# A wait for the stores of the new x moves from the end of the experts' stage to the state space's first load of a residual

## The reference

```
x = x + ga * attention(h)                      # layer 0, first half
h = layernorm(x) * (1 + cb) + sb
x = x + gb * experts(h)                        # layer 0, second half: gives the "new x"
h = layernorm(x) * (1 + ca) + sa               # layer 1
x = x + ga * state_space(h)                    # layer 1, first half
h = layernorm(x) * (1 + cb) + sb
x = x + gb * permuted_mlp(h)                   # layer 1, second half
```

## Time and profile before

| what | value |
|---|---|
| median of 3 runs | 1777.32 us (1776.28 to 1777.55) |
| the profiled execution's own time | 1780.89 us |
| its span on the core | 1779.1 us |
| PE busy | 1490.2 us (84%) |
| DVE busy | 1322.9 us (74%) |
| ACT busy | 1134.0 us (64%) |
| POOL busy | 924.0 us (52%) |
| DMA queue q1 (SP) | 163.81 MB, 34.3% of 16 engines |

### The profile page before, as it was taken

How to read it: one execution, slowest core, us unless ns; L and a number is a source line. 1 busy time by engine, 2 the same in 40 slices (tenths; PEclk the granted TensorE clock), 3 DMA queues, 4 the chain that set the end, 5 groups by cost and what they waited for, 6 DMA issues and landing times. The chain is left out here.

```text
span 1779.1 us, 26522 instructions
## 1 busy us (share of the span) xinstructions
PE 1490.2 (84%) x9052; PEld 815.1 (46%) x9052; DVE 1322.9 (74%) x2126; ACT 1134.0 (64%) x2277; POOL 924.0 (52%) x603
## 2 busy tenths in 40 slices
PE   5888999999978895678688898998989888755668
PEld 2441222222246443556365575665657566422432
DVE  3339999999056414107999999999999999999232
ACT  2323777777922233347788878878887887855138
POOL 0000000001010223326999999999999999999303
PEclk9875999999965897699799899999999999866689
DMA  6411112221072345823354554555554554644112
GB/s 247 160 43 42 28 32 81 79 81 59 3 231 95 101 137 206 290 69 87 96 137 114 132 136 118 129 122 118 135 130 119 125 125 108 137 101 112 68 51 95
DMA packets 154386, 199.10 MB, mean 112 GB/s; under 512 B 17567, under 2 KB 124999, under 8 KB 152716
## 3 DMA queue, kind: packets, MB, share of 16 engines
q1 hardware_dynamic: 142252, 163.81, 34.3%
q0 software_dynamic: 5168, 18.63, 3.2%
q10 hardware_dynamic: 6832, 14.96, 2.3%
HBM read 151.08 MB, written 46.28 MB: 111 GB/s over the span
## 5 line engine op out<-in xcount | busy, mean ns | idle before, releaser
L2040 DVE TENSOR_TENSOR_SCAN shared<-ssm_psum,ssm_state,shared 128x256 f32<-128x256 f32 x1024 | 674.9, 722 | 20.7 <-ACT ssm_state L1927 12.2
L1940 ACT ACTIVATE ssm_psum<-shared,ssm_a 128x256 f32<-128x256 f32 x1024 | 443.6, 468 | 157.7 <-DVE shared L2040 151.3
L1662 POOL TENSOR_TENSOR shared<-shared,ssm_bc 128x1024 f32<-128x1024 f32 x256 | 509.3, 2000 | 35.4 <-DVE shared L2040 16.0
L734 ACT ACTIVATE att_probs<-att_psum 128x1024 f32<-128x1024 f32 x256 | 248.3, 1021 | 75.2 <-PE att_psum L661 72.6
L1639 POOL TENSOR_TENSOR shared<-shared,ssm_bc 128x1024 f32<-128x1024 f32 x144 | 287.9, 1999 | 12.2 <-DMA shared<-drive_rows 12.2
L775 DVE TENSOR_REDUCE att_rowmax<-att_psum 128x1 f32<-128x512 f32 x448 | 277.5, 681 | 3.3 <-PE att_psum L634 1.5
L1765 PE MATMUL ssm_psum<-shared,ssm_select 128*32 128x256 f32 x2048 | 170.4, 423 | 93.9 <-POOL shared L1662 93.3
L603 POOL COPY att_v<-v_tokens 128x128 f32<-128x128 f32 x8 | 2.3, 292 | 298.8 <-ACT att_out L728 298.8
L634 PE MATMUL att_psum<-att_k,att_q 32*128 32x512 bf16 x448 | 138.0, 398 | 9.9 <-DVE att_rowmax L775 7.3
L1700 PE MATMUL ssm_psum<-ssm_h,late_weights 128*128 128x256 f32 x512 | 133.0, 421 | 9.3 <-ACT shared L1900 5.4
L673 PE MATMUL att_psum<-att_probs,att_v 128*32 128x512 f32 x1024 | 137.2, 608 | 0.6 <-ACT att_probs L734 0.6
(11 more groups left out here) (261 smaller groups left out, 1822.3 us busy)
## 6 DMA issues: line engine op xcount, KB each, us to landing
shared<-drive_rows SPq DMA_DIRECT2D x256, 256.0 KB, 4.5
qkv_wmod<-in_wmod SPq DMA_DIRECT2D x8, 1536.0 KB, 12.3
shared<-in_x SPq DMA_DIRECT2D x8, 1024.0 KB, 5.1
late_weights<-in_we SPq DMA_DIRECT2D x8, 1024.0 KB, 13.4
ssm_bc<-bc_rows SPq DMA_DIRECT2D x32, 256.0 KB, 5.2
drive_rows<-ssm_delta SPq DMA_DIRECT2D x64, 128.0 KB, 1.7
drive_rows<-ssm_du SPq DMA_DIRECT2D x64, 128.0 KB, 1.8
sorted_results<-moe_y ACTq DMA_DIRECT2D x23, 256.0 KB, 2.0
```

The lines of the kernel that those rows point to most:

```text
L734: nc.scalar.activation(probs[:, u % RING, :].rearrange("p (j t) -> p j t", j=2), ps_s[u % 2], ACT.Exp).then_inc(exp_done, 1)
L1662: nc.gpsimd.tensor_tensor(read(Q), drive(Q), bc[:, c % 2, 1, gr, :].unsqueeze(1).to_broadcast([P, J, SW]), ALU.mult).then_inc(read_done, 1)
L1940: nc.scalar.activation(ps_decay[n % HALF_BANKS][:, i], rep[:, s % 2, 0, j, :], ACT.Exp, scale=amat[:, t, gr, j:j + 1]).then_inc(decay_done, 1)
L2040: nc.vector.tensor_tensor_scan(drive(Q)[:, j, :], ps_decay[(2 * Q + j // 2) % HALF_BANKS][:, j % 2], drive(Q)[:, j, :], state[:, t, gr, j: ...
```

## The change

SP's block in `experts` no longer ends with the wait for the stores of the new x. The semaphore `x2_stored` becomes one of the shared ones, made in `build`, and `load_residual` waits for it before the first load.

```diff
--- before.py
+++ after.py
@@ -917,8 +917,8 @@
         srt_in = [sem(f"sorted{i}_in") for i in range(LOADS)]
         y_stored = [sem(f"y{i}_stored") for i in range(YSLOTS)]
         back_in = [sem(f"back{i}_in") for i in range(BACKS)]
-        x2_done, x2_stored, stat2_done, var2_done, sd2_done, rstd2_done, shift2_done, hn_dve, hn_act, hn_mm, hn_out = (sem(n) for n in (
-            "x2_done x2_stored stat2_done var2_done sd2_done rstd2_done shift2_done hn_dve hn_act hn_mm hn_out").split())
+        x2_done, stat2_done, var2_done, sd2_done, rstd2_done, shift2_done, hn_dve, hn_act, hn_mm, hn_out = (sem(n) for n in (
+            "x2_done stat2_done var2_done sd2_done rstd2_done shift2_done hn_dve hn_act hn_mm hn_out").split())
         block = ctx.enter_context(nc.Block())
         hdram = scratch.h.rearrange("(t p) f -> p t f", p=P)
         xdst = scratch.x2.rearrange("(t p) f -> p t f", p=P)
@@ -957,10 +957,9 @@
                 sp.dma_start(we[:, e], d["we"][e].rearrange("(k p) m -> p k m", p=P)).then_inc(experts_in, 16)
             for i in range(SCH):
                 sp.wait_ge(x2_done, (i + 1) * TC)
-                sp.dma_start(xdst[:, i * TC:(i + 1) * TC], x[:, i * TC:(i + 1) * TC]).then_inc(x2_stored, 16)
+                sp.dma_start(xdst[:, i * TC:(i + 1) * TC], x[:, i * TC:(i + 1) * TC]).then_inc(g.x2_stored, 16)
                 sp.wait_ge(hn_out, (i + 1) * TC)
                 sp.dma_start(hdst[:, :, i * SW:(i + 1) * SW], hnt[:, i % TSLOTS]).then_inc(g.hn_stored[i % TSLOTS], 16)
-            sp.wait_ge(x2_stored, 16 * SCH)
 
         @block.gpsimd
         def _(pool):
@@ -1567,6 +1566,8 @@
                     sp.dma_start(rep[32 * n:32 * n + 32, s % 2], src).then_inc(rep_in[s % 2], 16)
 
             def load_residual(c):
+                if c == 0:
+                    sp.wait_ge(g.x2_stored, 16 * SCH)
                 if c >= 1:
                     sp.wait_ge(out_mm, c * MP)
                 sp.dma_start(xres[:], xsrc[:, c * ST:(c + 1) * ST, :]).then_inc(xres_in, 16)
@@ -2231,6 +2232,7 @@
         g.att_used = []
         g.win_in = [ctx.enter_context(nc.semaphore(f"{n}_in")) for n in ("win_inner", "win_gate", "wout")]
         g.hn_stored = [ctx.enter_context(nc.semaphore(f"hn{s}_stored")) for s in range(TSLOTS)]
+        g.x2_stored = ctx.enter_context(nc.semaphore("x2_stored"))
         g.out_stored = [ctx.enter_context(nc.semaphore(f"out_{b}_stored")) for b in ("even", "odd")]
         g.ident = sb("ident", [P, P])
         g.run = sb("shared", [P, 2 * KT * T])
```

## The result

| | kernel before | changed kernel |
|---|---|---|
| median of 6 runs | 1777.18 us (1773.88 to 1779.87) | 1782.74 us (1778.22 to 1785.21) |
| span of the profiled execution | 1779.1 us | 1781.4 us |

The ratio is 1.0026, with a 95% interval from 1.0014 to 1.0038: slower by 4.6 us, or 2.5 to 6.8.

A forecast was written before the change was run, and what follows sets the result against it. The prediction took VectorE to hold the state space, so only its start matters; the load of h, sharing engines with the gate load, adds 4.0 us, other terms 0: 1777.32 + 4.0 = 1781.3 us, range 1776.3 to 1783.0.

The forecast's parts named there:

- The new wait costs 0: Ahead of the first residual load, issued at 931.4: the stores landed 201 us earlier, so the wait costs 0.
- The state space's instructions begin 4.0 us sooner: At the end of the experts' block: without SP's wait, instructions begin 4.0 us sooner where nothing else holds them.
- One for one: On the DMA engines: SP's and ACT's queues take turns packet by packet, whatever the packet size; chance 0.74.
- The reading by 4096 B: On the DMA engines: queues take turns of equal bytes, four 1 KB pieces per 4 KB one; 1779.6 us, chance 0.12.
- The modulation 4.1 us later: ACT's first modulation of h starts at 738.3 instead of 734.20, though everything is issued 4.0 us sooner.
- the late engine: One DMA engine of sixteen, with 2.0 us of stores left at 729.4; the others have up to 0.8 us.
- my own formula: Landing of the load of h: gate packets' start 729.4 + stores 2.0 + load 1.4 + gate load 5.2 = 738.0.
- The load right behind the stores: In SP's queue: the load of h follows the remaining stores, taking 1.4 us itself, in turns with gate packets.
- What follows costs 0: After the late load: the small weights, going out at 736.8, POOL's diagonals and W_out cost 0 each.
- The clock, 0, with 1.1 us as its dear end: PE's clock rise after its projections start: taken as 0; 3 us later costs 1.1, at once gives back 1.3.
- the main case: At the state space's start: one for one sharing, 4.0 us later, 1781.3 us; own range 1778.9 to 1782.5, chance 0.74.
- the load first: Rival: the load of h is served ahead of gate packets, 1.1 us sooner, 1776.2; chance 0.06 together with no change.

The follow-up runs named there:

- the repetition: The changed kernel profiled and timed again without any edit; ratio 1.0028 (1.0018 to 1.0038) to the kernel before.
- r6_warm: The changed kernel with 32 extra matmuls of PE behind its first eight, filling its wait for h; ratio 1.0025 to the kernel before.
- r2_gate_behind: The changed kernel with ACT's load of the gate half of W_in issued behind its first modulation; ratio 0.9992 to the kernel before.

## Why the prediction was right

I had forecast 1781.3 us; the ratio makes 1777.32 us into 1781.9. Point by point:

- *The new wait costs 0.* Right; the first residual load was issued at 936.7, 5.3 us later like all that is around it.
- *The state space's instructions begin 4.0 us sooner.* Right, 4.15 us.
- *One for one.* Right, and the step on which all hangs: 160 to 163 packets and 163 to 160. The reading by 4096 B that the Trainium skill allows ("DMA: Bandwidth & Descriptors", section "SWDGE vs HWDGE vs iDMA") gave 4 to 1, and the traces disagree.
- *The modulation 4.1 us later.* 3.6 in one execution and 5.5 in the other. But two terms of the sum were off. Gate packets came 3.3 us after their issue, at about 730.0, not 2.3: 1.0 us more. And the stores were nearly done by then: from 730.0 to 731.5 SP's queue ran 82 packets, where I had taken over the 212 of the earlier trace rows. The last store of normalised rows, which I had on the late engine until 736.7, had landed by 732.6, and SP's wait was 5.2 us, not 9. With the load landed at about 737.2 (0.3 us ahead of ACT's start at 737.48), my own formula leaves 737.2 - 730.0 - 1.4 - 5.2 = 0.6 us for these stores instead of 2.0, an estimate: 1.4 us less. The two errors nearly cancel, and that is luck.
- *The load right behind the stores.* Not so: from 730.5 to 731.5 SP's queue ran 18 packets beside 94 of the gate load. It cost little, since gate packets that had to run anyway ran in that time; the engines' share was 1.03 to 1.05 in every window from 730 to 736.
- *What follows costs 0.* Right: POOL began its diagonals at 738.16 and PE never waited for them.
- *The clock, 0, with 1.1 us as its dear end.* It was the dear end against the kernel before's 8.78 us, +1.1 and +1.2 us. Whether the longer idle did that is open, since four of the other kernels, with 3.5 to 6.7 us of idle, had 9.2 to 9.5 us too. With it the difference at the convolution is 4.7 us in the profiled execution, and 4.6 us is what the ratio gives.

So the mechanism and the main case held, but the closeness of 4.0 to 4.6 is in part luck: the modulation came 0.5 us less late than forecast in this execution and 1.4 us later than forecast in the other, and the clock added 1.1 us that I had at nothing. Two slips in the text change nothing: four microseconds before 731.14 is 727.14, not 727.12, and the range's lower end, the load first, is 1776.2 by its own sum, not 1776.3.

The bound of 0.2%, 3.55 us, lay in the middle of my forecast, and the measured 4.6 us is above it, with an interval that reaches below.

What stays open is why the load's packets came so late, some 5 us after SP's issue at 726.35, and later than the gate load's, which was issued 0.3 us behind it. The gap is there in the repetition (15 packets beside 87 from 731 to 732) and in r6_warm (11 beside 94 from 730.5 to 731.5), and not in r2_gate_behind, where SP's queue ran 607 packets at 94% of the engines from 730.2 to 732.2. So it comes with the early gate load. The length of the load's issue does not explain it: 0.97 us in the changed kernel instead of 0.36, but 0.98 in r2_gate_behind too.

## What to carry to other kernels

Before you remove a wait at a barrier, list every transfer that the barrier held back, not only the one at the head of the chain, and ask which of them will run beside the one that the chain needs. A queue of long packets beside a queue of short ones takes most of the engines' time, since they take turns by count (80% to 23% here, for 4 KB and 1 KB): issue the large load that is needed later behind the landing of the small one that is needed first. Then look at what else stands ahead of that one in its own queue.

## What the runs showed of the hardware

Two hardware queues with work on the same engines were served packet for packet, whether the short packets were of 128 B and less (182 to 193) or of 1 KB (160 to 163), each time beside packets of 4 KB. A load issued behind a backlog on its own queue, with a larger load issued 0.3 us later on another, left its queue all but empty for about 1 us (18 packets against 94) before its packets came; without that other load there was no such gap. And PE, idle for 11.25 us and then at work on the projections, had its clock raised 5.8 us after its start; with matmuls in that gap the clock was up before the projections began, and they took 6.9 to 7.0 us instead of 8.5 to 9.95.
